# Block 0's part of an attention kernel and what precedes it, put in another order

## The reference

```python
x = x + 0.5 * ffn(layernorm(x))      # base + shared + top-2-of-6 routed low-rank experts (rank 16)
x = x + attention(layernorm(x))      # 16 heads of 16, causal, layernorm of each head's q and k
x = x + 0.5 * ffn(layernorm(x))      # same weights as the first
```

## Time and profile before

| | us |
|---|---|
| median of 3 runs | 1210.83 (1210.62 to 1212.12) |
| the profiled execution | 1210.71 |
| its span | 1208.9 |
| TensorE busy | 1109.1 (92%) |
| ScalarE busy | 1016.4 (84%) |
| VectorE busy | 467.2 (39%) |
| POOL busy | 241.1 (20%) |

### The profile page before, as it was taken

The page is one execution under the profiler, slowest core; times in us unless marked ns, Lnnn a source line. Parts: engine busy times, 40 slices in busy tenths (PEclk is TensorE's granted clock), DMA queues, the critical chain, the costliest instruction groups (busy, mean ns, idle before and its releaser), DMA issues.

```text
span 1208.9 us, 22763 instructions
## 1 busy us (share of the span) xinstructions
PE 1109.1 (92%) x8884; PEld 359.0 (30%) x8884; DVE 467.2 (39%) x1177; ACT 1016.4 (84%) x1135; POOL 241.1 (20%) x377
## 2 busy tenths in 40 slices
PE   2557899999999999999999999999999999999985
PEld 2443433323333233232232222232222222221223
DVE  3676665753735354433432322331231212020214
ACT  3115688898988999999999999999999999999980
POOL 2234634313213211302021121011211101010100
PEclk9787899999999999999999999999999999999996
DMA  5002302002100310012100012000001100000000
GB/s 144 1 22 67 89 1 77 14 1 88 37 2 4 90 32 2 1 36 66 25 1 1 1 45 79 3 1 1 1 10 47 52 1 1 10 10 1 1 18 18
DMA packets 39672, 33.37 MB, mean 28 GB/s; under 512 B 8786, under 2 KB 39496, under 8 KB 39560
## 3 DMA queue, kind: packets, MB, share of 16 engines
q1 hardware_dynamic: 37360, 31.74, 8.9%
q10 hardware_dynamic: 2200, 0.12, 0.1%
HBM read 18.73 MB, written 12.85 MB: 26 GB/s over the span
## 4 chain that ended last, share of the span: by engine, by line
PE 71%; ACT 14%; DVE 7%; issue 5%; POOL 1%; ACTq 1%; DMA 0%; SPq 0%; DVEq 0%; POOLq 0%
PE ps L1179 67%; ACT ring L772 13%; PE ps L1221 2%; PE ps L1287 1%; DVE st L803 1%; PE ps L1241 1%; DVE area L824 1%; POOL rstd L713 0%; DVE xnT L844 0%; DMA x<-in_x 0%; POOL area L528 0%; POOL ring L726 0%; DVE tmp L789 0%; ACT area L761 0%; ACTq L737 0%
## 5 line engine op out<-in xcount | busy, mean ns | idle before, releaser
L772 ACT ACTIVATE ring<-ps 128x1024 f32<-128x1024 f32 x1056 | 983.4, 1112 | 68.0 <-PE ps L1179 66.5
L1179 PE MATMUL ps<-ring,vf 128*17 128x512 f32 (+3 forms) x4608 | 560.6, 564 | 2.3 <-ACT ring L772 0.8
L1179 PE MATMUL ps<-queries,keys 50*128 50x512 f16 (+3 forms) x2304 | 363.0, 366 | 22.2 <-ACT ring L772 4.4
L1179 PEld LDWEIGHTS ps<-queries,keys 50*128 50x128 f16 x2304 | 91.7, 93 | 472.6 <-ACT ring L772 433.1
L726 POOL TENSOR_SCALAR_AFFINE_SELECT ring<-ring 128x256 f32<-128x256 f32 (+1 forms) x224 | 103.1, 477 | 332.1 <-ACT ring L772 329.2
L1179 PEld LDWEIGHTS ps<-ring,vf 128*17 128x17 f32 x4608 | 79.8, 95 | 172.8 <-issue 144.3
L713 POOL TENSOR_TENSOR rstd<-var,minus_half 128x4 f32<-128x4 f32 x24 | 24.3, 1015 | 248.4 <-DVE var L809 248.1
L976 DVE SCALAR_TENSOR_TENSOR x<-ps,power,x 128x512 f32<-128x512 f32 x32 | 23.9, 750 | 118.2 <-PE ps L1179 118.2
L1179 PE MATMUL ps<-baseT,xnT 128*128 128x256 f16 x384 | 56.8, 289 | 1.3 <-DVE wf L850 1.3
L1148 DVE STREAM_TRANSPOSE oT<-ps 128x512 f32<-128x512 f32 x32 | 22.9, 716 | 89.4 <-PE ps L1179 88.7
L842 DVE CAST xnT<-ps 128x512 f16<-128x512 f32 x32 | 22.1, 689 | 91.0 <-PE ps L1221 91.0
(11 more groups left out here) (150 smaller groups left out, 677.6 us busy)
## 6 DMA issues: line engine op xcount, KB each, us to landing
parts_d<-split SPq DMA_DIRECT2D x32, 256.0 KB, 2.6
keys<-parts_d SPq DMA_DIRECT2D x96, 64.0 KB, 2.3
queries<-parts_d SPq DMA_DIRECT2D x192, 32.0 KB
x<-in_x SPq DMA_DIRECT2D x8, 512.0 KB, 4.3
out_x<-x SPq DMA_DIRECT2D x16, 256.0 KB, 2.2
queries<-shift_d SPq DMA_DIRECT2D x64, 4.0 KB
ring<-in_base_W SPq DMA_DIRECT2D x1, 256.0 KB, 4.1
ring<-in_Wq SPq DMA_DIRECT2D x1, 256.0 KB, 6.2
```

The source lines that it names most:

```text
L772: act.activation(probs[:, u % RING, :], bank(2 * (u % SLOTS), 2), ACTF.Exp, bias=0.0, scale=1.0).then_inc(exp_ok, 1)
L1179: return pe.matmul(o, lhsT, rhs, start=start, stop=stop, skip_group_check=True)
```

## The change

- spread() and together() go, and startup() is kept for another path through the kernel that these inputs don't take. In their place stands PRELUDE, a written string of 102 letters: w takes the next item of the weights (sizes and weight), f the next of the first feed-forwards of blocks 0, 1 and 2, p the next of prepare(0) and prepare(1), q the next fetch of block 0. The new prelude() yields them in that order, ahead of scores(0).
- 102 items stand ahead of the first scores where 89 stood. None moves behind. The 13 that move ahead are moments0, scale0 and turn0 of block 2 (two each), qk 7, square 7, squares 6 and 7, value (1, 0), and roots (1, 0) and (1, 1).
- Inside the prelude: sizes 0 comes ahead of scale0; weights 0, 1 and 2 ahead of inner0; sizes 1 ahead of weigh0; weight 3 ahead of outer0 of block 0; weight 4 behind moments1 of block 0, weight 5 behind the first scale0 of block 1, weight 6 behind squares 1 (all four stood behind outer0 and ahead of moments1). route0 (1, 1) and (1, 2) stand together ahead of value (0, 0), outer0 (1, 0) ahead of heads (0, 0), the heads 0, 2, 1 in a row; the four fetches of block 0 come behind all its heads.
- side_work() cuts from its lists what the prelude has taken; PLACES has new places for all that is left, in every block. In the first block's units there is left: the last root item, value (1, 1), norm 4 to 7, the heads, and block 2's feed-forward from inner0 on. Later blocks have the same items with places a few units off.

The diff, without the places of blocks 1 to 7:

```diff
--- before.py
+++ after.py
@@ -142,24 +142,15 @@
     yield 0, "load", c + XS
 
 
-def spread(items, first, last):
-
-    items = list(items)
-    total = sum(w for w, _, _ in items)
-    at, steps = 0.0, {}
-    for w, stage, n in items:
-        steps.setdefault(first + int(at / total * max(last - first, 1)), []).append((stage, n))
-        at += w
-    return steps
-
-
 def side_work(c):
 
     if c + 1 < NC:
 
-        yield "prep", list(itertools.chain(front(0, 0, c + 1) if c >= LONG else (), prepare(c + 1)))
+        taken = PRELUDE.count("p") - len(list(prepare(0))) if c == 0 else 0
+        yield "prep", list(itertools.chain(front(0, 0, c + 1) if c >= LONG else (), prepare(c + 1)))[taken:]
     if c + 2 <= LONG:
-        yield "ff", list(front(0, 0, c + 2))
+        taken = PRELUDE.count("f") - 2 * len(list(front(0, 0, 0))) if c == 0 else 0
+        yield "ff", list(front(0, 0, c + 2))[taken:]
     if c >= 1:
         yield "out", list(output(c - 1))
     behind = [c - 2] if 2 <= c < NC - 1 else [c - 2, c - 1] if c == NC - 1 else []
@@ -176,61 +167,63 @@
         yield from after.get((stage, n), [])
 
 
-def together(*lists):
-    steps = [spread(items, 0, 400) for items in lists]
-    for k in range(401):
-        for s in steps:
-            yield from s.get(k, [])
+
+PRELUDE = (
+    "ffwffwffwwffffwffwffppwfppfppfwfppppppffpppwpffpppffpppppffpppppfpppfppqpfppppppfqppfpqppfpfppppfppp"
+    "qp"
+)
 
 
 
 
 PLACES = {
-        (0, "prep"): (-1, -1, -1, -1, -1, -1, -1, -1, -1, -1, -1, -1, -1, -1, -1, 0, 1, 2, 3, 4, 4, 4, 7, 7, 8, 19, 19, 19, 21, 25, 36, 43),
-        (0, "ff"): (0, 2, 6, 9, 14, 19, 27, 30, 33, 36, 37, 46, 49, 55),
...
+        (0, "prep"): (0, 3, 12, 12, 12, 17, 21, 24, 34, 40),
+        (0, "ff"): (7, 19, 26, 31, 33, 46, 49, 54),
...
 }
 
 
+def prelude():
+    weights = [(0, "sizes", 0)] + [(0, "weight", k) for k in range(3)] + [(0, "sizes", 1)] + [(0, "weight", k) for k in range(3, NW)]
+    chains = {"w": iter(weights), "f": itertools.chain.from_iterable(front(0, 0, c) for c in range(3)),
+              "p": itertools.chain(prepare(0), prepare(1)), "q": ((0, "fetch", (0, g)) for g in range(NG))}
+    for k in PRELUDE:
+        _, stage, n = next(chains[k])
+        yield stage, n
+
+
 def schedule():
-    yield from startup()
-    for stage, n in together(prepare(0), front(0, 0, 1)):
-        yield stage, n
-        if stage == "heads" and n[1] in (2, 3):
-            for g in range(2):
-                yield "fetch", (0, 2 * (n[1] - 2) + g)
+    yield from prelude()
     side = {}
     for c in range(NC):
         for name, items in side_work(c):
             for (_, stage, n), place in zip(items, PLACES[c, name], strict=True):
                 side.setdefault(3 * UNIT0[c] + place, []).append((stage, n))
-    yield from side.pop(-1, [])
     yield "scores", 0
     yield "scores", 1
     values, groups, scored, split = [], [], set(), set()
```

More of the change, by code:

```diff
@@ L221, in schedule @@
-def schedule():
-    yield from startup()
-    for stage, n in together(prepare(0), front(0, 0, 1)):
-        yield stage, n
-        if stage == "heads" and n[1] in (2, 3):
-            for g in range(2):
-                yield "fetch", (0, 2 * (n[1] - 2) + g)
+PRELUDE = (
+    "ffwffwffwwffffwffwffppwfppfppfwfppppppffpppwpffpppffpppppffpppppfpppfppqpfppppppfqppfpqppfpfppppfppp"
+    "qp"
+)
+PLACES = {
+        (0, "prep"): (0, 3, 12, 12, 12, 17, 21, 24, 34, 40),
+        (0, "ff"): (7, 19, 26, 31, 33, 46, 49, 54),
+        (1, "prep"): (0, 3, 6, 9, 12, 18, 23, 24, 29, 30, 32, 32, 42, 42, 43, 48, 64, 64, 75, 76, 78, 79, 79, 90, 92, 95, 96, 97, 100, 101, 126, 135),
+        (1, "ff"): (12, 17, 26, 32, 36, 51, 56, 67, 102, 115, 130, 138, 145, 152),
+        (1, "out"): (28, 47, 73, 80),
+        (2, "prep"): (0, 15, 23, 23, 23, 35, 41, 53, 61, 64, 65, 66, 66, 85, 85, 86, 87, 96, 103, 120, 120, 126, 126, 138, 146, 146, 158, 161, 167,
+        201, 225, 245),
+        (2, "out"): (21, 27, 41, 47),
+        (2, "back"): (48, 49, 63, 68, 73, 92, 129, 135, 135, 135, 154, 160, 186, 192, 205),
+        (3, "prep"): (10, 26, 29, 32, 46, 53, 66, 76, 77, 78, 85, 89, 98, 111, 144, 155, 159, 160, 164, 175, 183, 184, 189, 192, 193, 193, 208, 210,
+        215, 215, 223, 227, 232, 244, 251, 254, 259, 264, 269, 271, 277, 282, 285, 295, 314, 337),
+        (3, "out"): (17, 24, 29, 40),
+        (3, "back"): (43, 51, 54, 63, 78, 129, 147, 166, 230, 230, 238, 238, 250, 271, 288),
+        (4, "prep"): (8, 31, 49, 50, 54, 71, 82, 100, 117, 117, 124, 140, 151, 163, 163, 167, 170, 171, 182, 195, 207, 207, 217, 224, 232, 234, 234,
+        236, 251, 256, 257, 262, 270, 301, 304, 317, 318, 318, 323, 332, 332, 349, 363, 387, 396, 430),
+        (4, "out"): (9, 9, 28, 36),
+        (4, "back"): (44, 61, 61, 81, 100, 107, 118, 183, 230, 236, 284, 286, 300, 338, 381),
+        (5, "prep"): (2, 20, 55, 63, 65, 78, 93, 97, 100, 101, 101, 113, 125, 141, 149, 149, 149, 176, 225, 236, 251, 253, 260, 276, 296, 296, 301,
+        324, 324, 324, 344, 344, 345, 360, 360, 364, 384, 387, 388, 398, 403, 434, 446, 456, 475, 533),
+        (5, "out"): (17, 27, 30, 48),
+        (5, "back"): (49, 67, 136, 156, 167, 183, 203, 323, 324, 325, 331, 368, 409, 514, 537),
+        (6, "prep"): (58, 58, 62, 62, 82, 98, 122, 139, 142, 146, 146, 156, 168, 196, 201, 224, 230, 230, 261, 281, 293, 300, 314, 324, 338, 348, 350,
+        356, 361, 381, 394, 408, 410, 446, 454, 457, 471, 482, 508, 508, 515, 517, 519, 558, 582, 609),
+        (6, "out"): (27, 27, 31, 63),
+        (6, "back"): (76, 114, 117, 132, 142, 216, 238, 296, 320, 339, 384, 428, 451, 539, 633),
+        (7, "out"): (31, 58, 69, 98),
+        (7, "back"): (121, 121, 124, 128, 131, 156, 188, 190, 195, 251, 251, 251, 342, 371, 375, 409, 409, 412, 431, 432, 443, 554, 554, 561, 602,
+        606, 652, 682, 719, 728),
+}
```

27 lines of the change are left out of this document (removed).

## The result

The changed kernel takes 1194.64 us (median, 1193.89 to 1196.64) beside 1210.72 for the kernel before: a ratio of 0.9863, 95% interval 0.9851 to 0.9875. I had forecast 1203.2 with a range of 1197 to 1210. The direction was right; the gain is 16 us where I had 7.6. The profiled execution took 1193.89 us, span 1192.1.

The account below looks back on a forecast made before the run. The loop was taken as full on TensorE and ScalarE, the start as bound by item order and waits. 1210.7 − 1.0 (first scores earlier) − 6.5 (first block's loop) = 1203.2 us, range 1197 to 1210.

Parts of the forecast that it names:

- Weights 3 to 6: Ahead of block 0's second moments: moving these weights' copies and subtractions away lets the moments start 4.06 us earlier.
- First feed-forward: Start of the prelude: sizes and weights 0 to 3 placed earlier lose 1.0 us, bounds 0 and 2.
- Projections to the last norm: Prelude: VectorE's 2.3 us of additions fit into 5.7 us of idle time; 0 us, bounds −1 and +2.5.
- the slower rival: Additions and collisions on VectorE's path, last stretch at 1.2 GHz: first scores 7.9 us late, 1216 us; chance 0.08.
- Heads: Last norm to last cast: outer0 (1, 0) ahead of all heads shortens it from 10.41 to 8.45 us.
- qk 4 to the scores: Last prelude stretch: four projections, two turns, one value take 11.9 us; first scores at about 101.8 us, 1.0 us earlier.
- The first block's loop: First block's 20 units: 4.3 us of TensorE work leaves, plus a third of the 6.3 us of waits; 6.5 us gained.
- Later positions: Later blocks: items shift by a few units, none added; nothing gained, bounds −2 and +2 us.
- The collisions: Prelude: four more VectorE products of two SBUF operands slowed beside POOL, 4 × 0.77 = 3.1 us; forecast 1206 with them.
- my seven signs: Profile windows: second moments, first projection, last norm, both first exponentials, TensorE's first-block clock (0.87 or above), ScalarE's waits (about 60 us).
- signs of being wrong: First exponential later than 106 us, first block's units still 38 us or more, or block 1's lead gone by 600 us.
- The rival that the stretch opens: First block: TensorE never idles long, clock stays at 2.4 GHz; prelude −2.5, loop −11 us, 1197 us; chance 0.16.

Follow-up runs that it names:

- e6: Changed kernel with weights 3 to 6 back in a row behind the first outer product and ahead of moments1: 1199.37 us, ratio 0.99.
- e18: The changed kernel as it is, run and profiled once more as a yardstick: 1194.99 us, ratio 0.9871.
- e16: Changed kernel with 76 unused 512-column products on TensorE in five gaps ahead of the loop: 1194.46 us, ratio 0.9856.
- e9: Changed kernel with outer0 (1, 0) back between heads (0, 0) and heads (0, 2): 1196.77 us, ratio 0.9876.
- e5: Changed kernel with the items left for the first block's units at the kernel before's places: 1197.61 us, ratio 0.989.
- e15: Changed kernel with sizes 0 behind scale0, weight 0 behind turn0, weights 1 and 2 behind the routing, as before: 1196.54 us, ratio 0.9878.
- e1: Kernel before with only the new order for its 89 prelude items, the 13 items and all places as before: 1201.4 us, ratio 0.9921.
- after: The changed kernel itself, here its profiled execution: median 1194.64 us, ratio 0.9863.
- e11: Changed kernel with the 13 items moved ahead standing in one row behind the other 89 instead of mixed in: 1203.17 us, ratio 0.9925.
- e3: Changed kernel with the kernel before's places for blocks 1 to 7: 1194.69 us, ratio 0.9866.
- e4: Kernel before with the changed kernel's places for blocks 1 to 7 alone: 1210.41 us, ratio 0.9991.
- e7: Changed kernel with 42 unused 512-column products on TensorE in three gaps ahead of the loop: 1196.85 us, ratio 0.9888.
- e14: Changed kernel with both moments0 of block 1 moved ahead of outer0 (0, 0): 1195.57 us, ratio 0.9864.
- e17: Changed kernel with block 1's moments0 ahead of outer0 (0, 0) and 72 unused TensorE products in five gaps: 1191.03 us, ratio 0.9831.

## Why the prediction was right and wrong

*What bounds the kernel*: right. The first block's units and the items ahead of them were where time could be won, the loop's body kept its pace, and the lead at block 1 was kept to the end.

*Weights 3 to 6*: right. 4.06 us by the sum, about 4.5 by e6.

*First feed-forward*: mis-sized. I had 1.0 us lost and second moments at 42.8; they came at 41.07, and at 41.96 in e18. So about 1 us was not lost; that any was gained isn't shown. I had left inner0 at the 2.54 us of the earlier trace rows. With weights 0 to 2 and the turns on TensorE right ahead of it, it took 1.41 us (1.41 and 1.47 in e18 and e16), as block 1's inner0 did before. That this is the clock is my reading of the two durations: the profile's column has 1.00 for inner0 in both kernels (24.96 to 27.3 us before, 24.65 to 26.06 after). It also began at 24.65 us where I had walked to 25.8.

*Projections to the last norm*: right. VectorE took the additions into its idle time, 21.72 us for 22.35, and had only 1.6 us left: the bound that I gave to the slower rival was near. The last norm came 0.8 us earlier than the 1.8 us that were already won at the second moments explain; no run says why.

*Heads*: right in mechanism (e9), wrong in size. I counted 8.45 us with the outer product at the low clock of the earlier trace rows; it was 7.06 with the high one, and e5 shows 8.2 with the low one.

*qk 4 to the scores*: mis-sized. I had 11.95 us, 4.9 more than before; measured 9.88, with 11.19 in e5 and 8.62 in e16. The term depends on the clock, and I had taken the kernel before's clock for it. Since the first block makes up for that clock (e9, e15), this term and the next are better judged together.

*The first block's loop*: mis-sized. 6.5 us by the sum, 8.1 measured; together with the term above, from qk 4 to the first exponential of block 1, 45.6 us by the sum, 41.99 measured. What the sum lacks there is a term for the new places of the items that stay in the first block: I had counted the items that leave and a third of the waits, and put the places at nothing without a reason. e5 puts them at 2.8 us in the trace and 3.3 in the median. Also, the 13 items cost 2.3 us ahead of the scores (e1 to after) and not 4.9, because they are mixed in (e11), which the sum doesn't name. TensorE's busy time in the block fell by 7.1 us, of which 4.3 were the products that I had counted; its clock there was 0.95 instead of 0.87, but that alone doesn't shorten the block: e1 has 0.96 and 38.5 us.

*Later positions*: right, nothing measurable (e3, e4).

*The collisions*: they came, though not to the products that I had named. Beside POOL's square L531 in after:

```profile
52.53 0.92 DVE L1050 TENSOR_SCALAR expo<-size 128x2 int32<-128x2 int32 x1
...
60.55 0.88 DVE L943 TENSOR_TENSOR eq<-eq,tri 128x144 bf16<-128x144 bf16 x1
```

The same two took 0.17 and 0.23 us before. Beside POOL stood also a cast (0.87 us for 0.17), L982 (0.73 for 0.41) and two scaling pairs (1.65 and 1.45, where one alone takes 0.72): 4.1 us in all, where the kernel before lost 1.2 us in this way ahead of its scores. That is some 2.9 us more on VectorE, an estimate from these rows, near the 3.1 us of my four. As the Trainium skill's rule has it (SBUF — State Buffer, section on who interferes with whom), of two operations that need the port pair shared by VectorE and POOL, the one issued second waits until the other is done; L943, with two SBUF inputs, agrees: it ended at 61.43 us, 0.1 us behind POOL's square. The norm came early all the same. How much of the 2.9 us lies on the chain no run shows; with only 1.6 us of idle time left on VectorE there, some of it may.

Added up: of the 9.3 us between my 1203.2 and the profiled 1193.89, 4.1 stood at qk 4 (1.8 by the second moments, 0.8 more by the last norm, 1.4 in the heads, 0.1 behind them), 3.6 came from there to block 1, and 1.6 behind it. Two steps failed. The larger is the term of the first block with what leads into it: it has nothing for the new places there, which e5 shows at about 3 us. The other is that I took the price of TensorE's work from its slow rows and carried it over into an order in which it ran faster: 1.1 us of inner0, and up to 1.4 us of the heads (1.2 by e5), where the granted clock was 0.76 before and 1.00 after. The same price is also part of the 2.1 us by which I had qk 4 to the scores too long, but in the runs with a low clock there the stretch as far as block 1 is no longer.

Of my seven signs, five moved further than I had allowed: the second moments, the first projection, the last norm and both first exponentials all came earlier than their windows. The first block's clock, 0.95, was in its window, and ScalarE's waits were 62.1 us for about 60. None of the signs of being wrong appeared. The rival that the stretch opens (1197, chance 0.16) was nearer to the time, but it had 2.5 us ahead of the scores and 11 in the block, where 7.2 and 8.1 were measured, so it had the place wrong.

What stays open: the 0.8 us ahead of the last norm and the 1.6 us behind the first block. Executions with one and the same loop behind block 1 scatter there by 2 us (1064.17 us in e18, 1066.22 in e7), so they may be nothing but chance.

## What to carry to other kernels

Where no engine is full, the order of independent chains sets the length: put one chain's work into the waits of another, item by item. The same 13 items cost 2.3 us mixed and 11 us in a row. Give the new places of what stays a term of their own, beside the items that leave. Price TensorE's work at both levels of its clock when a change fills or opens its gaps, and ask at the next meeting point of the engines whether the difference is still there; and look at a second execution of the same order before a difference of 2 us is laid to an edit.

## What the hardware showed that I had not expected

The same instructions ahead of the loop took 3.3 us longer in one profiled execution than in another (first exponential at 99.32 in e5, 96.05 in after, 97.12 in e18), with the granted clock in the same two stretches at 0.79 and 0.75 instead of 1.00 and 0.85. All executions have their mean clock on record, and it goes with the time: of the changed kernel's four, three with a mean clock of 0.980 took 1193.89 to 1194.97 us and the one with 0.975 took 1196.64; of e14's, two with 0.974 took 1196.3 and two with 0.980 and 0.981 took 1194.85 and 1193.8. That shows only that the two go together; what makes the clock differ stays open.

Feeding TensorE unused products through five gaps held the clock at 1.00 from 45 to 96 us and made the projections repeatable (4.04 us in e16 and e17); with three gaps filled it fell again behind the last. And alone the products gave nothing that can be measured (e16), alone the shortening of VectorE's chain gave nothing (e14), together they gave 4 us (e17). The intervals, some 2 us to either side, leave room for two small gains that add up, so that one lever needs the other isn't shown.
